# Newton squares of lane 0 on all four quadrants of the array, with a swapped second copy of image 1's iterate made on ScalarE

## What is computed

```
denom = max(sum(K, -2), -1)
V = 1/denom * K^T
for _ in range(6):
    KV = K @ V
    V = 0.25 * V @ (13 I - KV @ (15 I - KV @ (7 I - KV)))
out = (kernel_1 @ V) @ (kernel_3 @ v)
```

## Time and profile before

| | before |
|---|---|
| median of 3 runs | 721.57 us (721.25 to 721.74) |
| the profiled execution | 722.35 us, span 720.5 us |
| PE busy, PEld busy | 673.1 us (93%), 593.7 us (82%) |
| DVE busy | 494.9 us (69%) |
| ACT busy | 353.7 us (49%) |
| POOL busy | 107.3 us (15%) |
| squares, L371 from `rr` | 3840 matmul records, 130.1 us |
| products, L371 from `uu`, `qq` | 4608 matmul records, 96.5 us |

### The profile page before, as it was taken

One profiled execution on the slowest core, in us unless ns is written; L12 is line 12 of the kernel. 1 busy time (PEld: TensorE's weight loads), 2 busy tenths in 40 slices (PEclk: granted clock), 3 DMA queues, 4 the chain that ended last, 5 costly groups with the idle time before them and its releaser, 6 DMA issues.

```text
span 720.5 us, 29763 instructions
## 1 busy us (share of the span) xinstructions
PE 673.1 (93%) x13218; PEld 593.7 (82%) x13218; DVE 494.9 (69%) x1350; ACT 353.7 (49%) x916; POOL 107.3 (15%) x328
## 2 busy tenths in 40 slices
PE   5668999999999999999999999899999999999997
PEld 2557888888888888888888888778999999999996
DVE  5247777777887887778787887667547546646743
ACT  0124565555665665655665656655343443443442
POOL 0121222222222123122123131010000000000000
PEclk9969999999999999999999999999999999999999
DMA  8952111111111111110100000000000000000000
GB/s 310 308 192 61 63 33 32 62 33 34 62 33 34 62 33 35 60 33 32 62 4 4 5 4 5 4 2 1 1 0 23 1 1 23 1 0 23 1 1 22
DMA packets 12255, 30.63 MB, mean 43 GB/s; under 512 B 1120, under 2 KB 7392, under 8 KB 11616
## 3 DMA queue, kind: packets, MB, share of 16 engines
q1 hardware_dynamic: 12128, 28.73, 12.1%
HBM read 27.16 MB, written 1.57 MB: 40 GB/s over the span
## 4 chain that ended last, share of the span: by engine, by line
PE 77%; DVE 15%; ACT 4%; issue 2%; DMA 1%; POOL 0%; DVEq 0%; SPq 0%; POOLq 0%; ACTq 0%
PE ps L371 24%; PE ps L503 17%; PE ps L493 15%; PE ps L270 6%; DVE uu L761 4%; DVE sq L680 3%; PE ps L284 2%; PE ps L321 2%; PE ps L389 2%; PE ps L456 2%; ACT qq L574 2%; DVE rf L768 2%; PE ps L285 1%; ACT rr L578 1%; PE ps L382 1%
## 5 line engine op out<-in xcount | busy, mean ns | idle before, releaser
L820 DVE SCALAR_TENSOR_TENSOR acc<-ps,comb,acc 128x192 f32<-128x192 f32 x256 | 89.1, 410 | 83.9 <-PE ps L503 83.8
L503 PE MATMUL ps<-w_sb,work 128*128 128x192 f32 x768 | 140.4, 326 | 0.7 <-ACT work L651 0.7
L503 PEld LDWEIGHTS ps<-w_sb,work 128*128 128x128 f32 x768 | 129.5, 190 | 9.5 <-issue 1.1
L371 PE MATMUL ps<-rr 64*64 64x64 f32 x3840 | 130.1, 220 | 4.8 <-issue 2.1
L371 PEld LDWEIGHTS ps<-rr 64*64 64x64 f32 x3840 | 118.6, 135 | 17.5 <-ACT rr L578 10.8
L651 ACT ACTIVATE work<-ps 128x512 f32<-128x512 f32 x96 | 57.3, 597 | 137.8 <-PE ps L493 137.8
L574 ACT ACTIVATE qq<-ps 128x384 f32<-128x384 f32 x192 | 92.2, 489 | 63.4 <-PE ps L371 61.2
L761 DVE SCALAR_TENSOR_TENSOR uu<-rr,qq 128x384 f32<-128x384 f32 x160 | 87.8, 558 | 46.2 <-ACT qq L574 40.2
L578 ACT ACTIVATE rr<-ps 128x384 f32<-128x384 f32 x160 | 73.9, 489 | 80.3 <-PE ps L371 79.3
L371 PE MATMUL ps<-uu,qq 64*64 64x64 f32 x4608 | 96.5, 224 | 15.6 <-DVE uu L761 13.7
L371 PEld LDWEIGHTS ps<-uu,qq 64*64 64x64 f32 x4608 | 80.5, 134 | 33.4 <-DVE uu L761 30.2
(11 more groups left out here) (137 smaller groups left out, 1032.5 us busy)
## 6 DMA issues: line engine op xcount, KB each, us to landing
xtb<-xt_dram SPq DMA_DIRECT2D x16, 512.0 KB, 3.6
work<-x_dram SPq DMA_DIRECT2D x16, 512.0 KB, 3.7
wsh<-ws_dram SPq DMA_DIRECT2D x2, 1440.0 KB, 7.7
w_sb<-w_dram SPq DMA_DIRECT2D x1, 2304.0 KB, 25.8
w_a<-w_dram SPq DMA_DIRECT2D x1, 1536.0 KB, 12.5
w_b<-w_dram SPq DMA_DIRECT2D x2, 768.0 KB, 16.7
out_dram<-acc SPq DMA_DIRECT2D x4, 384.0 KB, 2.6
mult<-copies_dram SPq DMA_DIRECT2D x1, 512.0 KB, 13.0
```

Of the source, the lines that this page charges most:

```text
L371: last = pe.matmul(ps[z:z + 64, 2 * lane + i, 64 * j:64 * j + 64], lhs[r, lane, i, j, :], rhs[r, lane, i, j, :], start=True, stop=True)
L503: last = pe.matmul(ps[:, 2 + 2 * (e % 2) + j // 2, (j % 2) * DIM:(j % 2 + 1) * DIM], hid[:, n % 4, j * P:(j + 1) * P], w2_sb[:, c, :], sta ...
L820: last = dve.scalar_tensor_tensor(out=a, in0=ps[:, 2 + 2 * (e % 2) + j // 2, (j % 2) * DIM:(j % 2 + 1) * DIM], scalar=comb[:, g * GT + j, ...
```

## The change

In lane 0 the squares of image 1 too write to the other half (`crossed`), so that lane 0's squares use all four quadrants. Lane 1 is as before. `qq` of lane 0, image 1, now has its halves swapped against `rr`, so the sum needs `rr` with halves swapped: `r0` and `rr` get a third slot beside the two images (index 2; only lane 0 uses it), and `swap_halves` fills it with two ScalarE copies of 64 partitions x 192 columns, from 0..63 to 64..127 and back, out of slot 1 in SBUF. VectorE's `newton_sum` of lane 0 reads slots 0 and 2 (`0:3:2`) and waits for `swapped` as well. The product crosses once more, so that lane 0's image 1 comes back to the half it had.

`swap_halves(0, t)` stands at the head of ScalarE's `iteration(t)`; `swap_halves(k + 1, t)` stands behind rr of lane 1 and ahead of the second window of step k. There are 12 copies for each of the 16 tiles.

```diff
-        r0 = sb("r0", [P, 2, 2, LP, 64])
-        rr = sb("rr", [P, 2, 2, LP, 64])
+        r0 = sb("r0", [P, 2, 3, LP, 64])
+        rr = sb("rr", [P, 2, 3, LP, 64])
...
-                            z = 64 * (half ^ (i * phase))
+                            crossed = i == 1 and (phase == 1 or lane == 0)
+                            z = 64 * (half ^ crossed)
...
+            def swap_halves(k, t):
+                src = r0 if k == 0 else rr
+                if k == 0:
+                    act.wait_ge(r0_ready, 2 * t + 1)
+                else:
+                    act.wait_ge(r_ready, 12 * t + 2 * k - 1)
+                for a in (0, 64):
+                    act.activation(src[64 - a:128 - a, 0, 2].rearrange("p h n -> p (h n)"),
+                                   src[a:a + 64, 0, 1].rearrange("p h n -> p (h n)"), ACT.Copy).then_inc(swapped, 1)
...
             def iteration(t):
                 for k in range(STEPS):
+                    if on(t) and k == 0:
+                        swap_halves(0, t)
                     if on(t):
                         newton(k, 0, t, 0)
                         newton(k, 0, t, 1)
...
                         newton(k, 1, t, 0)
                         newton(k, 1, t, 1)
+                    if on(t) and k < STEPS - 1:
+                        swap_halves(k + 1, t)
                     second_window(k, t)
...
                 dve.wait_ge(q_ready, n + 1)
-                dve.scalar_tensor_tensor(out=uu[:, lane], in0=src[:, lane], scalar=3.0, in1=qq[:, lane],
+                if lane == 0:
+                    dve.wait_ge(swapped, 12 * t + 2 * k + 2)
+                dve.scalar_tensor_tensor(out=uu[:, lane], in0=src[:, lane, 0:3:2] if lane == 0 else src[:, lane, 0:2], scalar=3.0, in1=qq[:, lane],
```

More of the change, by code:

```diff
@@ L147, in vit_block_kernel @@
         y_copied, square_done = sems("y_copied square_done")
-        q_ready, u_ready, prod_done, r_ready, o_done = sems("q_ready u_ready prod_done r_ready o_done")
+        swapped, q_ready, u_ready, prod_done, r_ready, o_done = sems("swapped q_ready u_ready prod_done r_ready o_done")
         o_copied, proj_done, h2_ready = sems("o_copied proj_done h2_ready")
@@ L577, in newton @@
                     act.wait_ge(prod_done, n + 1)
-                    act.activation(rr[:, lane].rearrange("p i h n -> p i (h n)"), ps[:, 2 * lane:2 * lane + 2, 0:LC],
+                    act.activation(rr[:, lane, 0:2].rearrange("p i h n -> p i (h n)"), ps[:, 2 * lane:2 * lane + 2, 0:LC],
                                    ACT.Copy, scale=0.25).then_inc(r_ready, 1)
+            def swap_halves(k, t):
[7 more added lines that the diff above has]
+                                   src[a:a + 64, 0, 1].rearrange("p h n -> p (h n)"), ACT.Copy).then_inc(swapped, 1)
             def copy_out(t):
@@ L752, in start_newton @@
                 for lane in range(2):
-                    dve.tensor_tensor(r0[:, lane].rearrange("p i h n -> p i (h n)"),
+                    dve.tensor_tensor(r0[:, lane, 0:2].rearrange("p i h n -> p i (h n)"),
                                       eye3.unsqueeze(1).to_broadcast([P, 2, LC]),
```

## The result

| | before | changed |
|---|---|---|
| median of 5 runs | 721.57 us (721.24 to 721.74) | 733.04 us (730.51 to 734.44) |
| ratio | | 1.0157 (95%: 1.0136 to 1.0178) |
| the profiled execution | 722.35, span 720.5 | 734.04, span 732.0 |
| PE busy | 673.1 | 654.6 |
| ACT busy | 353.7 | 413.6 |

The forecast was 723.1, range 714 to 726. The sign was right, the size was not: +11.5 us instead of +1.5. The last two lines of the table are read from the timeline of TensorE, from the start of one square of `r` to the next. All but 0.5 us of the loss lie in the Newton phase: +7.2 in iterations 0 to 12, +3.8 in the last three.

What follows compares the result with a forecast made beforehand. TensorE led the Newton phase, with VectorE setting the pace in some stretches. -0.8 us over 13 iterations and +2.3 in the last three gave +1.5: 723.1 against 721.57, range 714 to 726.

Steps and rivals of the forecast that it cites:

- what the squares save: TensorE, Newton phase: lane 0's square falls to 0.43 us, 0.345 less in each of 96 steps, 33 us in all.
- gains in steps 2, 3 and 5 alone: Only these Newton steps can use the faster squares, together about 1 us an iteration if nothing else moved.
- Rival C: Crossed squares don't run together: nothing saved, copies paid, +0.45 us an iteration, about +3 at the end, 730; chance 0.05.
- The price of the copies: ScalarE behind rr of lane 1: copies of 0.345 us without overlap, the pair delaying what follows by 0.86 us.
- B: ScalarE copies overlap throughout: pair at 0.50 us, -0.95 an iteration, 709.4 us; chance 0.10.
- rival A: Only one side's partition change costs ScalarE overlap: pair at 0.73 us, -0.50 an iteration, 716.1 us; chance 0.28.
- The walk through an iteration: Start times followed through steps 0 to 5 of a full Newton iteration: -0.06 us each, times 13, -0.8.
- the one on step 2: Column sums start at 234.03 instead of 233.42, VectorE free 1.12 later, u of step 3 at 235.15 instead of 235.23.
- the 0.09 walked: TensorE's squares of step 2 move only 0.09 us, to 228.46.
- TensorE's idle time in the phase near 55 us: Newton phase: idle time rises from 20.9 to near 55 us, since what TensorE saves is waited away.
- +0.7 was forecast: Last Newton iteration, t = 15, where ScalarE stands in the chain itself: +0.7 us.
- the walked +0.6 and +1.0: Iterations t = 13 and t = 14, thin windows with ScalarE in the chain: +0.6 and +1.0 us.

Runs made afterwards that it cites:

- cross_only: Changed kernel without the ScalarE copies and VectorE's wait for them, lane 0's squares still crossed, part of the computation wrong: 706.4 us, ratio 0.9797 to before.
- pool_after: Changed kernel with GpSimd's residual and low_tokens made to wait until VectorE has written r0 of the next tile in step 4: 729.0 us, ratio 1.0102 to before.
- warm2: pool_after with extra unused TensorE matmuls ahead of lane 0's product, three in step 0 and two in step 4: 725.9 us, ratio 1.0049 to before.
- copies_only: Changed kernel with the ScalarE copies and the wait, but lane 0's squares uncrossed and VectorE reading unswapped slots: 738.4 us, ratio 1.0231 to before.
- order_reversed: Changed kernel with the two ScalarE copies in reverse order, upper half to lower first: one execution, 741.0 us.
- res_again: Changed kernel with GpSimd's residual alone moved behind r0, low_tokens left in place, second try: 735.5 us, ratio 1.0198 to before.

## Why the prediction was wrong

- **The bound, and what the squares save: right.** Squares at 1.20 us a step as worked out, gains in steps 2, 3 and 5 alone: cross_only's products of these steps start 0.36, 0.71 and 1.07 us earlier. Rival C (squares don't run together) is refuted.
- **The price of the copies: near, but not as reasoned.** Duration 0.36 instead of 0.345. The pair costs 0.78 ahead of readers of PSUM and 0.90 ahead of readers of SBUF, instead of 0.86 everywhere. B is refuted. Both sides count, but the read side only among operations that read SBUF, so ahead of copy_kernel, copy_x2 and copy_xl two overlaps are lost and not three. That is rival A's count; with copies of 0.36 us its price would be 0.76. A's iteration (0.50 us shorter) did not come even with the collisions out, in part since squares behind copy_xl loses its overlap as well: in pool_after copy_xl is 0.60 us later than before and q of step 5 0.74.
- **The walk through an iteration: right in its order, wrong in one assumption.** It carried every VectorE operation along at its old duration. The failed sentence is the one on step 2, "column sums at 234.03 instead of 233.42, and VectorE is free 1.12 after their start": the start of the sums was right to 0.03 us, and what ran behind them met GpSimd's residual. The same happened to u of step 4. GpSimd was not looked at at all. With its operations moved (pool_after, warm2) the iteration is 26.5, as forecast; with them in place it is 27.13, some 0.6 us more in each undisturbed iteration, the largest part of the error. The forecast length of 26.50 is in part luck: the pair is 0.08 cheaper than assumed in steps 2 and 3, and the product of step 2 comes 0.14 later than walked.
- **A smaller slip in it:** where lane 1's product waits for its u, the two products start 0.47 us apart instead of 0.40. With it TensorE's squares of step 2 start 0.23 us later and not the 0.09 walked, and the product of step 2 comes -0.12 instead of -0.26. In the full iteration it didn't decide.
- **"TensorE's idle time in the phase near 55 us": near in number (50.8), and its consequence missed.** The number is not the forecast's sum: TensorE was busy 18 us less, not 33, and the phase was 11 us longer. The text treated the idle time as merely waited away. In the profiled execution the clock fell, which cost 2.4 us in iteration 12; the second fall lies in the last iteration, which came out at +2.25 where +0.7 was forecast (3.4 us at half the clock can be at most 1.7 of that, an estimate). The scatter goes with the clock: the two runs at 0.989 and 0.991 took 730.5 and 731.6 us, the three at 0.978 to 0.986 took 733.0 to 734.4, where before had 721.2 to 721.7. So even with the clock up the loss is 9 to 10 us. Iterations 13 and 14 came out at +0.55 and +0.98, near the walked +0.6 and +1.0; in 14 a u stretched to 0.88 us and a pause of 0.61 are in it, so that agreement is partly luck.
- **What stays open.** warm2, with both disturbances nearly out, is +3.9 us where +1.5 was forecast. Its iterations 0 to 12 sum to the same as before (+0.1, forecast -0.8), its last three to +4.3 (forecast +2.3), in which lie 3.4 us at the lower clock and u's of up to 1.1 us beside the moved GpSimd operations. I have not separated these. What makes TensorE pause in step 4 no run shows. Nor does any run tell how many falls of the clock a given load brings: they differ from run to run of one kernel.

The range of 714 to 726 was built on the price of the copies alone. Both things that broke it, the stretched VectorE operations and the clock, stood in the sum at nothing, so no bound on its terms could have covered them.

## What to carry to other kernels

When a change moves an engine's work by half a microsecond, look at what every other engine does at the new time, GpSimd's elementwise operations against VectorE's first of all: a walk that keeps durations fixed is only half a walk. Work taken off TensorE counts only where TensorE was late, and what it then idles can cost the clock. A copy that moves data between partition halves costs its full duration, so put such copies where their engine idles, and drop the steps in which they buy nothing.

## What the hardware showed that was not expected

**VectorE and GpSimd hold each other up.** A 128x192 tensor_scalar went from 0.37 to 0.80 us with a GpSimd operation of 0.61 beside it, and a 128x384 sum of two SBUF operands from 0.56 to between 0.81 and 1.10. It goes the other way too: in the changed kernel a residual of GpSimd's at 428.85 took 1.44 us instead of 0.60, behind two u's that kept their 0.55. A reduction out of PSUM with 0.28 us of the residual beside it kept its 0.69 (copies_only, from 236.63). By the Trainium skill (SBUF — State Buffer, SBUF: two separate sides) the two engines share a pair of SBUF ports as an exclusive lock, which VectorE takes in its two-port modes and with two inputs from SBUF; the trace agrees in kind: the sum has two inputs from SBUF, the tensor_scalar one input and its output there (64 columns take 0.31 us and 192 take 0.37, so 128 more cost 0.06), and it ended 0.12 us after GpSimd's operation did. The recorded starts don't tell who is held up, though: the tensor_scalar is recorded 0.07 us ahead of the residual and is the one stretched, while the residual takes 0.61 us against 0.60 before.

**ScalarE loses its overlap of some 0.1 us** when the first written partition changes, and when the first partition read in SBUF differs from that of the last operation that read SBUF, even with a reader of PSUM between them (copy_xl to squares, 0.26 to 0.39 us). By the Trainium skill (ScalarE: Activation LUTs, What ACT_TABLE_LOAD costs) back-to-back activations overlap by about 93 ns; the trace agrees where the partitions stay (two rr of 0.49 us start 0.39 apart) and disagrees where they change (two copies of 0.36 start 0.39 apart).

**TensorE's clock fell in mid-kernel** from 2.4 to 1.2 GHz, mostly for 3.4 or 6.8 us at a time (once 10.2, in order_reversed), in kernels where it had been busy 379 and 381 of the 430 us, and not in the profiled phase of one with 399 of 430. Ahead of the falls shown it had been busy 9.68 of 11.0 us and 10.62 of 12.2, and had just stood still for 1.17 and 1.21 us. Iterations with a fall of 6.8 us and no pause took 2.4 and 3.1 us more than the others of their kernel (changed, res_again), those with a pause of 1.2 to 1.3 us as well 3.4 to 4.3 us more.
